# Gated cross-attention with a quantised feed-forward: inputs of feed-forward groups 2 to 4 transposed by DMA instead of TensorE

## The chip, the cores and the metric

The kernel runs on one core of one Trainium2 chip. The metric is device time in microseconds (us), the median of several executions. One execution is also recorded by the hardware profiler; all durations of single instructions come from that one.

## What is computed

The input x is 16 batches of 128 rows by 512 columns. A cross-attention block adds to it, and a feed-forward block adds to the result. The change lies in the second:

```python
x = x + jnp.tanh(g_xattn[0]) * _L0_xattn_ref(_layernorm(x, axis=-1), ctx_2048, ...)
x = x + jnp.tanh(g_ffn[0]) * _L0_ffn_ref(_layernorm(x, axis=-1), ...)

def _L0_ffn_ref(x, gate_up_packed, gate_up_scales, down_packed, down_scales):
    I = gate_up_packed.shape[0] // 2                       # 1408
    gate_up = jnp.einsum('bsh,oh->bso', x, w_gu)           # w_gu: fp4 values times scales
    gate, up = (gate_up[..., :I], gate_up[..., I:])
    h = jax.nn.silu(gate) * up
    y = jnp.einsum('bsi,hi->bsh', h, w_down)
    rms = jnp.sqrt(jnp.mean(y * y, axis=-1, keepdims=True) + EPS)
    return y / rms
```

## The kernel before

Attention takes the first 420 us. The feed-forward stage works on four groups of four batches (GROUP = 4), counted 0 to 3 in the code (g) and 1 to 4 in this text. Each group goes through IT = 11 steps, one for each 128 of the 1408 inner columns; T_ counts all 44 steps and t the step inside its group.

In a step TensorE does, in this order: 16 matmuls of 128x512 for gate and up (`gate_up`, L404, four input slices k, each with the head and the rest of the input in half precision), and 12 matmuls of 128x512 for the down product of step T_ - 2 (`project_down`, L420). Gate and up share four PSUM banks. ScalarE reads the gate banks (`take_gate`, L318), applies silu (L325) and makes the head of the hidden values (L331). VectorE reads the up banks (`take_up`, L167 and L170), multiplies (`join`, L175) and makes the rest of the hidden values (`hidden_rest`, L181). GpSimd adds the four gate parts (L299, L303).

Between these stands the work on the next and the last group, at fixed steps t: statistics of the next group (t = 1 to 4), its normalisation on GpSimd into `xn` (t = 5 and 6, `normalise`, L223), and for the last group the copy of y (t = 2), squares (t = 3, 4), the gain (t = 5) and the final sum on VectorE (`finish`, t = 6 to 9, L254), whose four results SyncE stores (`store`, L159).

The matmuls need the normalised input with its columns on the partitions, split into a half-precision head and a half-precision rest. Before the change this was done at t = 7 to 10 (TURN_AT = 7) for the next group: after the gate and up matmuls of the step TensorE transposes four 128x128 squares of `xn` into PSUM bank 0 (`turn_inputs`, L387), ScalarE copies the bank as the head (`input_head`, L335), VectorE subtracts the head from the bank (`input_rest`, L228), and the first gate matmul of the following step waits for that rest. There are two sets of head and rest tiles, used in turn. Each engine runs its instructions in the order of the code; semaphores tie the engines together. SyncE's queue holds, at the end of the attention, the last transfers of batch 15 and then the stores of the four groups.

Of the kernel before, what the change touches and what calls it, by code (L numbers as in the profile page):

```python
# [7 lines left out]
ALU = mybir.AluOpType  # L8
ACT = mybir.ActivationFunctionType
# [4 lines left out]
F16 = mybir.dt.float16  # L14
# [24 lines left out]
GROUP = 4  # L39
# [14 lines left out]
GROUPS = B // GROUP  # L54
# [4 lines left out]
H_RING = 3  # L59
STATS_AT, EVAC_AT, SQUARE_AT, ROOT_AT, NORM_AT, OUT_AT, TURN_AT = 1, 2, 3, 5, 5, 6, IT - KT  # L60
STEP_ROWS = 6
# [40 lines left out]
def feed_forward(nc, ctx, d, keep, tiles):  # L102
# [50 lines left out]

    turn_bank = lambda g, k: 0 if g else k

# [62 lines left out]
    def normalise(engine, ops, g, j):  # L218
        engine.wait_ge(negated, g + 1)
        engine.wait_ge(inv, g + 1)  # L220
        if g:
            engine.wait_ge(turned, g * KT)
        ops.tensor_scalar(xn[:, j, :], xg[g][:, j, :], neg_mean[:, j:j + 1], rstd[:, 1, j:j + 1],  # L223
                          ALU.add, ALU.mult).then_inc(normed, 1)

    def input_rest(dve, g, k):
        dve.wait_ge(x_heads, g * KT + k + 1)
        nc.vector.tensor_tensor(x_rest[g % 2][:, k], gu_ps[turn_bank(g, k)], x_head[g % 2][:, k], ALU.subtract).then_inc(x_rests, 1)  # L228

    def first_input_head(dve, k):  # L230
        dve.wait_ge(turned, k + 1)
        nc.vector.tensor_copy(x_head[0][:, k], gu_ps[turn_bank(0, k)]).then_inc(x_heads, 1)

# [23 lines left out]
    def vector_step(dve, T_):  # L257
# [11 lines left out]
        if T_ < NT:  # L269
            take_up(dve, T_, 3)  # L270
        if g + 1 < groups and t >= TURN_AT:
            input_rest(dve, g + 1, t - TURN_AT)
        if drains:
# [58 lines left out]

    def input_head(act, g, k):
        act.wait_ge(turned, g * KT + k + 1)
        nc.scalar.activation(x_head[g % 2][:, k], gu_ps[turn_bank(g, k)], ACT.Copy).then_inc(x_heads, 1)  # L335

# [13 lines left out]
    def scalar_step(act, T_):  # L350
# [9 lines left out]
        if T_ < NT:  # L360
            take_gate(act, T_, 2)
            take_gate(act, T_, 3)
        if g + 1 < groups and t >= TURN_AT:
            input_head(act, g + 1, t - TURN_AT)
        if drains:
# [14 lines left out]

    def turn_inputs(pe, g, k):
        if k == 0:
            pe.wait_ge(normed, (g + 1) * GROUP)
        if g:
            pe.wait_ge(gate_read, 4 * ((g - 1) * IT + TURN_AT + k) + 3)
        for j in range(GROUP):
            last = nc.tensor.transpose(gu_ps[turn_bank(g, k)][:, j * P:(j + 1) * P], xn[:, j, k * P:(k + 1) * P], keep["ident"][:])  # L387
        last.then_inc(turned, 1)

    def gate_up(pe, T_, n):  # L390
# [3 lines left out]
        at = 4 * T_ + k  # L394
        if t > TURN_AT and g + 1 < groups and n == 0:
            pe.wait_ge(x_rests, (g + 1) * KT + t - TURN_AT)
        elif at >= 2:
            pe.wait_ge(up_read if is_up else gate_read, at - 1)
        if T_ == 0 and n < KT:
            pe.wait_ge(x_rests, n + 1)  # L400
        elif t == 0 and n == 0:
            pe.wait_ge(x_rests, (g + 1) * KT)
        for moving, first in ((x_head, True), (x_rest, False)):
# [4 lines left out]
    def project_down(pe, T_):  # L408
# [3 lines left out]
        for j in range(GROUP):  # L412
# [14 lines left out]
            "turn_inputs": turn_inputs, "gate_up": gate_up, "project_down": project_down, "scalar_step": scalar_step,  # L427
            "last_squares": last_squares, "statistics": statistics, "normalise": normalise, "input_rest": input_rest,
            "first_input_head": first_input_head, "vector_step": vector_step, "last_finish": last_finish,
# [3 lines left out]
def attend(nc, d, keep):  # L433
    with ExitStack() as ctx:
# [115 lines left out]
        with ExitStack() as attention:  # L550
# [22 lines left out]
        with nc.Block() as block:  # L573
# [161 lines left out]
            def _(sp):  # L735
# [123 lines left out]
            def tensor_step(pe, b):  # L859
                for slot in range(SLOTS):  # L860
# [315 lines left out]
            def _(dve):  # L1176
# [171 lines left out]
```

## Time and profile before

| | |
|---|---|
| median of 3 runs | 721.06 us (720.33 to 721.33) |
| the profiled execution | 721.24 us, span of its instructions 719.4 us |
| TensorE busy | 688.7 us, 96% |
| VectorE busy | 610.1 us, 85% |
| ScalarE busy | 519.3 us, 72% |
| GpSimd busy | 476.3 us, 66% |
| mean granted TensorE clock | 0.974 of full speed |

Busy is the time in which an engine has an instruction at work. Matmuls are pipelined and overlap in the record, so how fast TensorE goes is better read from the distance between the same instructions of two steps. PEld is TensorE's loading of weights, which runs beside its matmuls (PE). An instruction's idle time, in brackets in a timeline, is how long its engine did nothing before it, with the instruction that ended the wait.

### The profile page before, as it was taken

What the parts mean: (1) busy time and instruction counts of PE and PEld (TensorE: products, weight loads), DVE (VectorE), ACT (ScalarE), POOL (GpSimd) and SP (SyncE); (2) the same over time, 40 slices, a digit from 0 to 9 for tenths busy, and PEclk for the clock granted to TensorE, in tenths of its full rate; (3) what the DMA queues carried; (4) which work ended last, traced back from release to release, by engine and by line L of the source; (5) the groups of instructions that cost most, each with busy time, mean ns of one, the idle gap of its engine ahead of it and who ended that gap; (6) DMA issues with size and microseconds to landing.
All of it is one profiled execution on the core that took longest, in us unless ns stands there. A gap on an engine that the chain in (4) does not pass through costs nothing.

```text
span 719.4 us, 13389 instructions
## 1 busy us (share of the span) xinstructions
PE 688.7 (96%) x4678; PEld 338.4 (47%) x4678; DVE 610.1 (85%) x825; ACT 519.3 (72%) x925; POOL 476.3 (66%) x403
## 2 busy tenths in 40 slices
PE   3779999999999999999999999999999999999995
PEld 2334434443444344434444344665565556555653
DVE  6788988988898889888989879776899789977894
ACT  1228888888888888888888976566666666666653
POOL 3857655796779766966633239976697669766773
PEclk8659999999999999999999999999999999999999
DMA  8787777778877877878663311000001000100001
GB/s 250 179 204 164 174 195 201 176 182 207 200 170 188 208 200 176 201 200 194 160 150 71 86 50 48 0 1 1 0 10 37 15 1 9 37 16 0 10 37 73
DMA packets 48935, 80.59 MB, mean 112 GB/s; under 512 B 14436, under 2 KB 17892, under 8 KB 48868
## 3 DMA queue, kind: packets, MB, share of 16 engines
q1 hardware_dynamic: 47712, 78.99, 43.7%
q10 hardware_dynamic: 1156, 0.74, 0.4%
q8 instruction: 37, 0.61, 0.4%
q14 instruction: 30, 0.25, 0.1%
HBM read 45.11 MB, written 32.24 MB: 108 GB/s over the span
## 4 chain that ended last, share of the span: by engine, by line
PE 48%; POOL 30%; issue 16%; DVE 3%; DMA 2%; ACT 1%; POOLq 0%; SPq 0%; DVEq 0%; ACTq 0%
PE pv_ps L845 18%; POOL probs L299 15%; PE s_ps L815 13%; POOL probs L303 9%; PE st_ps L827 8%; PE st_ps L788 2%; PE st_ps L800 2%; PE st_ps L857 2%; PE st_ps L794 2%; DVE max_rows L1119 1%; DMA qk_stack<-image 1%; POOL proj L1051 1%; POOL over_stack L223 1%; POOL proj L1046 1%; POOL cross L1044 1%
## 5 line engine op out<-in xcount | busy, mean ns | idle before, releaser
L1119 DVE TENSOR_REDUCE max_rows<-s_ps 128x2 f32<-128x1024 f32 x256 | 304.0, 1212 | 37.4 <-PE s_ps L815 36.7
L956 ACT ACTIVATE probs<-st_ps 128x512 f32<-128x512 f32 x512 | 278.1, 598 | 56.4 <-PE st_ps L827 46.0
L318 ACT ACTIVATE probs<-s_ps,gu_sc 128x512 f32<-128x512 f32 x176 | 117.7, 685 | 84.4 <-PE s_ps L404 84.2
L299 POOL TENSOR_TENSOR probs<-probs 128x512 f32<-128x512 f32 x88 | 120.3, 1371 | 69.5 <-ACT probs L318 69.3
L845 PE MATMUL pv_ps<-probs,v_all 128*32 128x256 f32 x2048 | 163.5, 392 | 0.6 <-ACT pv_all L962 0.6
L815 PE MATMUL s_ps<-qk_stack 48*128 48x512 f32 x512 | 132.7, 515 | 7.8 <-DVE max_rows L1119 5.3
L170 DVE SCALAR_TENSOR_TENSOR proj<-s_ps,gu_sc,proj 128x512 f32<-128x512 f32 x132 | 98.7, 748 | 11.1 <-PE s_ps L404 1.9
L827 PE MATMUL st_ps<-qk_stack 50*128 50x512 f32 x512 | 106.8, 405 | 0.0
L420 PE MATMUL st_ps<-dn_head,over_input 128*128 128x512 f32 x264 | 104.9, 423 | 1.0 <-DVE over_input L181 1.0
L815 PEld LDWEIGHTS s_ps<-qk_stack 48*128 48x128 f32 x512 | 49.3, 190 | 112.5 <-issue 73.8
L1081 POOL TENSOR_TENSOR heads_out<-pv_all,scale_of 128x512 f32<-128x512 f32 x16 | 20.5, 1282 | 98.0 <-DMA scale_of<-inverse_scratch 89.2
L404 PE MATMUL s_ps<-pv_all,gu_bits 128*128 128x512 f16 x352 | 80.1, 380 | 0.2 <-DVE proj L167 0.2
L845 PEld LDWEIGHTS pv_ps<-probs,v_all 128*32 128x32 f32 x2048 | 40.6, 108 | 84.3 <-ACT probs L956 59.9
L303 POOL TENSOR_TENSOR probs<-probs 128x512 f32<-128x512 f32 x44 | 71.3, 1622 | 3.5
L404 PE MATMUL s_ps<-split_head,gu_bits 128*128 128x512 f16 x176 | 66.9, 380 | 1.9 <-DVE proj L167 1.5
L827 PEld LDWEIGHTS st_ps<-qk_stack 50*128 50x128 f32 x512 | 64.8, 187 | 6.7 <-issue 3.4
L404 PE MATMUL s_ps<-split_rest,gu_bits 128*128 128x512 f16 x176 | 66.7, 379 | 0.0
L167 DVE TENSOR_SCALAR proj<-s_ps,gu_sc 128x512 f32<-128x512 f32 x44 | 32.8, 746 | 31.9 <-PE s_ps L404 31.8
L420 PEld LDWEIGHTS st_ps<-dn_head,over_input 128*128 128x128 f32 x264 | 49.6, 188 | 17.3 <-ACT over_input L331 1.4
L1044 POOL TENSOR_TENSOR cross<-proj,sin 128x1024 f32<-128x1024 f32 x15 | 35.7, 2379 | 30.0 <-ACT proj L946 27.2
L404 PEld LDWEIGHTS s_ps<-pv_all,gu_bits 128*128 128x128 fp8e3 x352 | 32.1, 98 | 43.4 <-issue 5.9
L420 PE MATMUL st_ps<-dn_rest,over_input 128*128 128x512 f32 x132 | 52.0, 394 | 0.0
(122 smaller groups left out, 892.2 us busy)
## 6 DMA issues: line engine op xcount, KB each, us to landing
qk_stack<-image SPq DMA_DIRECT2D x60, 384.0 KB, 6.4
image<-split_rest SPq DMA_DIRECT2D x32, 256.0 KB
image<-split_head SPq DMA_DIRECT2D x31, 256.0 KB
image<-split_head SPq DMA_DIRECT2D x62, 128.0 KB
xt_all<-x_dram SPq DMA_DIRECT2D x16, 256.0 KB, 3.6
ct<-ctx_dram SPq DMA_DIRECT2D x16, 256.0 KB, 3.6
scale_of<-inverse_scratch SPq DMA_DIRECT2D x16, 256.0 KB
out_dram<-over_stack SPq DMA_DIRECT2D x16, 256.0 KB, 2.0
```

The source lines that it names most:

```text
L170: nc.vector.scalar_tensor_tensor(out, bank, scale, out, ALU.mult, ALU.add).then_inc(up_read, 1)
L299: nc.gpsimd.tensor_tensor(pair[:, n], parts[T_ % 2][:, 2 * n], parts[T_ % 2][:, 2 * n + 1], ALU.add).then_inc(pairs_ok, 1)
L303: nc.gpsimd.tensor_tensor(gate[T_ % 2], pair[:, 0], pair[:, 1], ALU.add).then_inc(gate_ok, 1)
L318: nc.scalar.activation(parts[T_ % 2][:, k], gu_ps[(2 * k) % BANKS], ACT.Copy, scale=gu_sc[:, k, T_ % IT:T_ % IT + 1]).then_inc(gate_read, 1)
L404: last = nc.tensor.matmul(gu_ps[n % BANKS], gu_vals[:, k, col:col + P], moving[g % 2][:, k], start=first, stop=not first)
L420: last = nc.tensor.matmul(y_ps[j], h[T_ % H_RING][:, cols], keep[w][:, t, :], start=(t == 0 and n == 0), stop=(t == IT - 1 and n == 2))
L815: last = nc.tensor.matmul(out[:, odd, :], q_stack[p][rows, j, qt * P:(qt + 1) * P], k_stack[p][rows, j, :], start=True, stop=True)
L827: nc.tensor.matmul(out[:], k_stack[p][rows, j, kt * P:(kt + 1) * P], q_stack[p][rows, j, :], start=True, stop=True).then_inc(st_full, 1)
L845: last = nc.tensor.matmul(pv_ps[2 * KC * j:2 * KC * (j + 1), cols], v_ones[b % 2][:, kt, j, quad, :], probs[at % PROBS][:, j, cols], start ...
L956: nc.scalar.activation(probs[at % PROBS][:, tile % 4, :], st_ps[item % ST_BANKS][:], ACT.Exp).then_inc(st_read, 1)
L1044: ops.tensor_tensor(cross[:], tile[:], sin[:], ALU.mult).then_inc(crossed, 1)
L1119: nc.vector.tensor_reduce(out, s_ps[item % S_BANKS][:], AXIS_X, ALU.max).then_inc(s_read, 1)
```

## The change

For groups 2 to 4 TensorE's transposes into PSUM go. At t = 6 to 9 (SPLIT_AT = 6) ScalarE copies a batch of `xn` in half precision into `flat_head`, and VectorE subtracts that from `xn` into `flat_rest`, both in SBUF with the columns still along the row. SyncE then issues for each of the four batches four transposing transfers of 128x128 from `flat_head` and four from `flat_rest` into the head and rest tiles: 32 transfers in a group. The first gate matmul of the group waits until all 32 have landed. The order of SyncE's queue becomes: transposing transfers of group 2, those of group 3, stores of group 1, transfers of group 4, stores of group 2, stores of groups 3 and 4. The first group is still transposed by TensorE. `flat_head` and `flat_rest` lie over tiles that the attention stage used.

```diff
-STATS_AT, EVAC_AT, SQUARE_AT, ROOT_AT, NORM_AT, OUT_AT, TURN_AT = 1, 2, 3, 5, 5, 6, IT - KT
+STATS_AT, EVAC_AT, SQUARE_AT, ROOT_AT, NORM_AT, OUT_AT, SPLIT_AT = 1, 2, 3, 5, 5, 6, 6
...
-    turn_bank = lambda g, k: 0 if g else k
+    TURNS = 16 * 2 * KT * GROUP
...
     def normalise(engine, ops, g, j):
...
-        if g:
-            engine.wait_ge(turned, g * KT)
+        if g == 1:
+            engine.wait_ge(turned, KT)
+        elif g:
+            engine.wait_ge(flat_rests, (g - 1) * GROUP)
...
-    def input_rest(dve, g, k):
-        dve.wait_ge(x_heads, g * KT + k + 1)
-        nc.vector.tensor_tensor(x_rest[g % 2][:, k], gu_ps[turn_bank(g, k)], x_head[g % 2][:, k], ALU.subtract).then_inc(x_rests, 1)
+    def flat_input_rest(dve, g, j):
+        dve.wait_ge(flat_heads, (g - 1) * GROUP + j + 1)
+        if g >= 2:
+            dve.wait_ge(turned_in, TURNS * (g - 1))
+        nc.vector.tensor_tensor(flat_rest[:, j], xn[:, j, :], flat_head[:, j], ALU.subtract).then_inc(flat_rests, 1)
+
+    def turn_by_dma(sp, g):
+        sp.wait_ge(up_done, 4 * (g - 1) * IT)
+        for j in range(GROUP):
+            for out, flat, done in ((x_head, flat_head, flat_heads), (x_rest, flat_rest, flat_rests)):
+                sp.wait_ge(done, (g - 1) * GROUP + j + 1)
+                for k in range(KT):
+                    sp.dma_start(out[g % 2][:, k, j * P:(j + 1) * P], flat[:, j, k * P:(k + 1) * P], transpose=True).then_inc(turned_in, 16)
...
-        if g + 1 < groups and t >= TURN_AT:
-            input_rest(dve, g + 1, t - TURN_AT)
+        if T_ < NT and g + 1 < groups and SPLIT_AT <= t < SPLIT_AT + GROUP:
+            flat_input_rest(dve, g + 1, t - SPLIT_AT)
...
-    def input_head(act, g, k):
-        act.wait_ge(turned, g * KT + k + 1)
-        nc.scalar.activation(x_head[g % 2][:, k], gu_ps[turn_bank(g, k)], ACT.Copy).then_inc(x_heads, 1)
+    def flat_input_head(act, g, j):
+        act.wait_ge(normed, g * GROUP + j + 1)
+        if g >= 2:
+            act.wait_ge(turned_in, TURNS * (g - 1))
+            act.wait_ge(flat_rests, (g - 2) * GROUP + j + 1)
+        nc.scalar.activation(flat_head[:, j], xn[:, j, :], ACT.Copy).then_inc(flat_heads, 1)
...
-        if g + 1 < groups and t >= TURN_AT:
-            input_head(act, g + 1, t - TURN_AT)
+        if T_ < NT and g + 1 < groups and SPLIT_AT <= t < SPLIT_AT + GROUP:
+            flat_input_head(act, g + 1, t - SPLIT_AT)
...
-        if t > TURN_AT and g + 1 < groups and n == 0:
-            pe.wait_ge(x_rests, (g + 1) * KT + t - TURN_AT)
-        elif at >= 2:
+        if at >= 2:
             pe.wait_ge(up_read if is_up else gate_read, at - 1)
         if T_ == 0 and n < KT:
             pe.wait_ge(x_rests, n + 1)
-        elif t == 0 and n == 0:
-            pe.wait_ge(x_rests, (g + 1) * KT)
+        elif t == 0 and n == 0 and g:
+            pe.wait_ge(turned_in, TURNS * g)
...
+            "flat_head": magnitude[:].bitcast(F16)[:, 0:GROUP * T].rearrange("p (j t) -> p j t", t=T),
+            "flat_rest": dn_bits[:].bitcast(F16)[:, 0:GROUP * T].rearrange("p (j t) -> p j t", t=T),
...
                 for g in range(GROUPS):
-                    ffn["store"](sp, g)
+                    if g + 1 < GROUPS:
+                        ffn["turn_by_dma"](sp, g + 1)
+                    if g:
+                        ffn["store"](sp, g - 1)
+                ffn["store"](sp, GROUPS - 1)
...
-                if g + 1 < GROUPS and t >= TURN_AT:
-                    ffn["turn_inputs"](pe, g + 1, t - TURN_AT)
```

## Rows read from the trace of the kernel before

**Rows 1.** The page: busy time of two engines; TensorE's granted clock in 40 slices.
```profile
PE 688.7 (96%) x4678; PEld 338.4 (47%) x4678; DVE 610.1 (85%) x825; ACT 519.3 (72%) x925; POOL 476.3 (66%) x403
PEclk8659999999999999999999999999999999999999
```

**Rows 2.** Windows, busy us by engine: a plain step, and steps 18 and 19.
```profile
492.80:499.10 6.30, 6.30 (x30) 3.79 (x30) 4.52 (x6) 3.74 (x6) 3.97 (x4) 1.00 0.01 3
...
537.00:544.30 7.30, 6.94 (x34) 4.06 (x34) 6.91 (x8) 4.28 (x7) 7.14 (x7) 1.00 0.10 37
544.30:551.30 7.00, 6.80 (x33) 3.92 (x32) 6.79 (x10) 4.28 (x7) 5.09 (x4) 1.00 0.10 37
```

**Rows 3.** Timeline of weight loads: start us, duration; first loads of steps 6, 7, 11.
```profile
459.74 0.10 PEld L404 LDWEIGHTS s_ps<-split_head,gu_bits 128*128 128x128 fp8e3 x1 [0.27 <-issue]
...
466.01 0.10 PEld L404 LDWEIGHTS s_ps<-split_head,gu_bits 128*128 128x128 fp8e3 x1 [0.28 <-issue]
...
492.81 3.14 PEld L404 LDWEIGHTS s_ps<-pv_all,gu_bits 128*128 128x128 fp8e3 x16 [0.27 <-issue]
```

**Rows 4.** The same timeline, steps 17 to 22, loads that waited.
```profile
530.71 3.13 PEld L404 LDWEIGHTS s_ps<-pv_all,gu_bits 128*128 128x128 fp8e3 x16 [0.27 <-issue]
...
536.96 1.84 PEld L404 LDWEIGHTS s_ps<-pv_all,gu_bits 128*128 128x128 fp8e3 x10 [0.27 <-issue]
...
540.95 0.42 PEld L387 LDWEIGHTS s_ps<-ident,over_stack 128*128 128x128 f32 x4 [0.85 <-POOL over_stack L223]
...
544.25 1.84 PEld L404 LDWEIGHTS s_ps<-pv_all,gu_bits 128*128 128x128 fp8e3 x10 [0.28 <-issue]
546.79 0.54 PEld L404 LDWEIGHTS s_ps<-pv_all,gu_bits 128*128 128x128 fp8e3 x4 [0.69 <-DVE proj L167]
...
564.73 0.10 PEld L404 LDWEIGHTS s_ps<-split_head,gu_bits 128*128 128x128 fp8e3 x1 [0.27 <-issue]
```

**Rows 5.** Groups by form, 440 us to the end: count, busy us, mean ns.
```profile
L181 DVE TENSOR_TENSOR over_input<-cross,over_input 128x512 fp32r<-128x512 f32 x43 | 39.8, 925 | 1.7 <-ACT over_input L331 0.7
...
L254 DVE SCALAR_TENSOR_TENSOR over_stack<-over_stack,rms,xt_all 128x512 f32<-128x512 f32 x4 | 7.0, 1758 | 0.0
...
L335 ACT ACTIVATE pv_all<-s_ps 128x512 f16<-128x512 f32 x8 | 4.8, 597 | 1.7 <-PE s_ps L387 1.7
...
L254 DVE SCALAR_TENSOR_TENSOR over_stack<-st_ps,rms,xt_all 128x512 f32<-128x512 f32 x3 | 2.2, 747 | 0.1
```

**Rows 6.** Timelines of VectorE: step 9, then steps 17 to 22.
```profile
484.14 0.69 DVE L228 TENSOR_TENSOR pv_all<-s_ps,pv_all 128x512 f16<-128x512 f32 x1
...
531.79 0.75 DVE L167 TENSOR_SCALAR proj<-s_ps,gu_sc 128x512 f32<-128x512 f32 x1 [0.30 <-PE s_ps L404]
...
542.88 1.51 DVE L181 TENSOR_TENSOR over_input<-cross,over_input 128x512 fp32r<-128x512 f32 x1
...
546.00 0.74 DVE L167 TENSOR_SCALAR proj<-s_ps,gu_sc 128x512 f32<-128x512 f32 x1
...
550.22 0.68 DVE L181 TENSOR_TENSOR over_input<-cross,over_input 128x512 fp32r<-128x512 f32 x1
...
552.51 0.74 DVE L167 TENSOR_SCALAR proj<-s_ps,gu_sc 128x512 f32<-128x512 f32 x1
...
565.81 0.75 DVE L167 TENSOR_SCALAR proj<-s_ps,gu_sc 128x512 f32<-128x512 f32 x1 [1.75 <-PE s_ps L404]
```

**Rows 7.** Timeline of ScalarE: the last two gate copies of step 9.
```profile
482.02 1.31 ACT L318 ACTIVATE probs<-s_ps,gu_sc 128x512 f32<-128x512 f32 x2
```

**Rows 8.** SyncE's issues by line: ns min/median/max; landing after L646.
```profile
L159 SPq DMA_DIRECT2D out_dram<-over_stack x16: 332/332/377, 538.3 to 716.9; - x16
...
L646 SPq DMA_DIRECT2D pv_all<-pv_all x64: 571/589/1847, 77.9 to 427.9; - x64
DMA to landing us min/median/max: 1.9/3.2/4.7
...
L664 SPq DMA_DIRECT2D x_scratch<-xt_all x8: 533/990/1663, 119.2 to 287.3; - x8
```

More of the change, by code:

```diff
@@ L118, in feed_forward @@
     gu_ps, y_ps = tiles["gu_ps"], tiles["y_ps"]
+    flat_head, flat_rest = tiles["flat_head"], tiles["flat_rest"]
     rms = sb("rms", [P, 4, GROUP], F32)
@@ L127, in feed_forward @@
     turned = sem("turned3")
+    flat_heads = sem("flat_heads")
+    flat_rests = sem("flat_rests")
+    turned_in = sem("turned_in")
     x_heads = sem("x_heads")
@@ L220, in normalise, with first_input_rest @@
         engine.wait_ge(inv, g + 1)
-        if g:
-            engine.wait_ge(turned, g * KT)
+        if g == 1:
+            engine.wait_ge(turned, KT)
+        elif g:
+            engine.wait_ge(flat_rests, (g - 1) * GROUP)
         ops.tensor_scalar(xn[:, j, :], xg[g][:, j, :], neg_mean[:, j:j + 1], rstd[:, 1, j:j + 1],
                           ALU.add, ALU.mult).then_inc(normed, 1)
-    def input_rest(dve, g, k):
-        dve.wait_ge(x_heads, g * KT + k + 1)
-        nc.vector.tensor_tensor(x_rest[g % 2][:, k], gu_ps[turn_bank(g, k)], x_head[g % 2][:, k], ALU.subtract).then_inc(x_rests, 1)
+    def flat_input_rest(dve, g, j):
[10 more added lines that the diff above has]
+                    sp.dma_start(out[g % 2][:, k, j * P:(j + 1) * P], flat[:, j, k * P:(k + 1) * P], transpose=True).then_inc(turned_in, 16)
+    def first_input_rest(dve, k):
+        dve.wait_ge(x_heads, k + 1)
+        nc.vector.tensor_tensor(x_rest[0][:, k], gu_ps[k], x_head[0][:, k], ALU.subtract).then_inc(x_rests, 1)
     def first_input_head(dve, k):
         dve.wait_ge(turned, k + 1)
-        nc.vector.tensor_copy(x_head[0][:, k], gu_ps[turn_bank(0, k)]).then_inc(x_heads, 1)
+        nc.vector.tensor_copy(x_head[0][:, k], gu_ps[k]).then_inc(x_heads, 1)
     def wait_y(engine, g, j):
@@ L379, in last_squares, with turn_inputs @@
             square(act, groups - 1, j, y_ps[j])
-    def turn_inputs(pe, g, k):
+    def turn_inputs(pe, k):
         if k == 0:
-            pe.wait_ge(normed, (g + 1) * GROUP)
-        if g:
-            pe.wait_ge(gate_read, 4 * ((g - 1) * IT + TURN_AT + k) + 3)
+            pe.wait_ge(normed, GROUP)
         for j in range(GROUP):
-            last = nc.tensor.transpose(gu_ps[turn_bank(g, k)][:, j * P:(j + 1) * P], xn[:, j, k * P:(k + 1) * P], keep["ident"][:])
+            last = nc.tensor.transpose(gu_ps[k][:, j * P:(j + 1) * P], xn[:, j, k * P:(k + 1) * P], keep["ident"][:])
         last.then_inc(turned, 1)
@@ L427, in feed_forward @@
             "turn_inputs": turn_inputs, "gate_up": gate_up, "project_down": project_down, "scalar_step": scalar_step,
-            "last_squares": last_squares, "statistics": statistics, "normalise": normalise, "input_rest": input_rest,
+            "last_squares": last_squares, "statistics": statistics, "normalise": normalise, "first_input_rest": first_input_rest, "turn_by_dma": turn_by_dma,
             "first_input_head": first_input_head, "vector_step": vector_step, "last_finish": last_finish,
@@ L880, in tensor_step @@
                             pe.wait_ge(s_read, B * SLOTS)
-                        ffn["turn_inputs"](pe, 0, slot - FIRST_TURN)
+                        ffn["turn_inputs"](pe, slot - FIRST_TURN)
             def tensor_feed(pe, T_):
@@ L1217, in _ @@
                     ffn["first_input_head"](dve, k)
-                    ffn["input_rest"](dve, 0, k)
+                    ffn["first_input_rest"](dve, k)
                 dve.wait_ge(scales_ok, 2)
```

## The prediction

> **What bounds the kernel now.** The page first: TensorE is busy 96% of the span, VectorE 85%, and the granted clock is at its upper level in every slice but the first few [rows 1]. The change touches only the feed-forward stage, steps T_ = 0 to 43 from 422 us on, so the rest was read by step; groups are counted 1 to 4 here, steps by T_. The table of windows shows a plain step (492.8 to 499.1) with TensorE busy throughout and VectorE at 4.52 of 6.30 us, and steps T_ = 18 and 19 (537.0 to 551.3) in which VectorE fills 6.8 to 6.9 us and TensorE has gaps [rows 2]. I then took the start of each step from TensorE's weight loads: the load of the first gate matmul follows a short "issue" pause. Group 1: step 6 runs from 459.74 to 466.01, 6.27 us; the four steps with transposes from 466.01 to 492.81, 26.80 us or 6.70 each [rows 3]. A plain step is 6.25 us (530.71 to 536.96), so four transposes and their detour cost 0.45 us per step, bound by TensorE itself. In group 2 the same five steps run 530.71, 536.96, 544.25, 551.33 to 564.73, 34.02 us in all, where 5 x 6.25 + 4 x 0.45 would be 33.05. The difference has two names: the transposes of step 18 wait 0.85 us for GpSimd's normalised rows, and step 19 waits 0.69 us for VectorE to read a bank [rows 4]. I take group 3, which has the same work at the same t, to be alike.
>
> **What goes.** 48 transposes, four in each of twelve steps, with their copies out of PSUM. In group 1 VectorE has room, so the whole 4 x 0.45 = 1.8 us comes back. In groups 2 and 3 the bound is 34.02 - 31.25 = 2.8 us each, if TensorE alone sets the pace.
>
> **What VectorE and ScalarE do instead.** They execute as many splits as before, one step earlier, and now from SBUF: the head on ScalarE about 0.6 us [rows 5], the rest on VectorE. Of the rest's new form no row exists. Bounds: 0.69 us as now from PSUM [rows 6]; 0.92 us, the mean of L181, a TENSOR_TENSOR with both inputs in SBUF; 1.76 us, the time of L254 with both inputs in SBUF, against 0.75 when one is in PSUM [rows 5]. I take 0.69: L181 is the same operation and runs at 0.68 when nothing holds it [rows 6].
> The move matters in groups 2 and 3. VectorE's `finish` (1.76 us) stands in t = 6 to 9, the split in t = 7 to 10, so both meet in three steps now and in all four after. Such a step takes VectorE 552.51 - 546.00 = 6.51 us, more than TensorE's 6.25. From its first read of step 17 at 531.79, four of them end at 557.83. TensorE feels it when the first read, naturally 1.08 us into a step (565.81 against 564.73), starts after 1.35: the bank is wanted again ten matmuls or 2.2 us in, and the read takes 0.75. Step 21 would start at 530.71 + 25.0 = 555.71, so it is held 557.83 - 557.06 = 0.8 us, and step 22 starts at 562.8: 2.0 us gained. In step 18 L181 took 1.51 us instead of 0.68 [rows 6] while GpSimd was late with the normalisation; if that repeats, 1.1 us are gained. I take 1.4 per group, nearer to this end since GpSimd's work doesn't change, and 2.8 for two. Sum of the compute side: 1.8 + 2.8 = 4.6 us. The ends are 1.8 + 2 x 2.8 = 7.4 and, with the rest at 0.92 in four steps (0.9 less per group) and the slow step, 2.
>
> **What the transfers cost.** 32 transposing transfers per group are issued one by one by SyncE, each 128x128 in half precision, 32 KB. None is in the trace. They cost TensorE nothing if all have landed at the first gate matmul of the next group, the only wait that the change adds there; behind it on TensorE stand gate, up and down products, so every microsecond late is a microsecond of span. ScalarE ends its last gate copy 3.9 us into a step (482.02 + 1.31 = 483.3 against 466.01 + 2 x 6.70 = 479.4) and the head takes 0.6 [rows 7], so SyncE starts 4.5 us into t = 6; GpSimd's last normalised rows are there when the transposes of step 18 start, 540.95 [rows 4], ahead of the splits that need them in steps 19 and 20. SyncE's other waits, on up products of two groups back and on its own earlier transfers, are over by then. With a pace r per transfer and a landing L after the last issue, the last lands at 4.5 + 31r + L; group 1 allows 31.25 us, groups 2 and 3 32.6. What else bounds it: the last rest is ready 5.4 us into t = 9 (484.14 + 0.69 - 479.4 [rows 6]), with four transfers to issue and 12.5 - 5.4 = 7.1 us left.
> Rows for r: a plain 256 KB issue in this stage holds SyncE 0.33 us; the copies from SBUF to SBUF of 32 KB each, the nearest in place and size, 0.59 us, with a landing of 1.9 to 3.2; slow ones in the attention stage 0.99 (median of L664) to 1.85 (longest of L646) [rows 8]. With 0.59 and 3.2 the last lands at 26.0, and the tail rule gives 5.4 + 4 x 0.59 + 3.2 = 11.0 of 12.5 us: hidden. In this stage the queue is otherwise empty, which is why I take 0.59 and not the slow rows. Hidden holds up to r = 0.80 (L = 2.0). Beyond it each 0.1 us costs 3.1 us per group. All of the 4.6 us is eaten at about r = 0.87.
> Here the Trainium skill speaks with two voices. "VectorE: DVE Perf Modes", section "The three transpose paths", gives 1309 ns for one 128x128 transpose by DMA against 390 ns by TensorE; no run here shows whether that is a pace or a time to completion. As a pace it would put the last landing near 47 us and the time near 761, an estimate from that page. "Advanced Engine Details and Errata", section "X-Bar Transpose (TRN2)", says that such DMAs are as fast as regular ones, by which the sum above stands.
> **SyncE's queue.** The stores of group g - 1 now stand behind the transfers of group g + 1. Their first reader is ScalarE's square in step 36, which reuses `y_out` some fifteen steps later; the last group's stores have nothing new ahead of them. Nothing.
>
> **Sum.** The profiled execution took 721.24 us, 719.4 in its span and 1.8 around it, 0.2 above the median of the runs. 721.24 - 1.8 - 2.8 = 716.6.
>
> **Rivals.**
> - A, the forecast: r under 0.8, hidden, 716.6 us, from 714 (TensorE alone sets groups 2 and 3) to 719.5 (VectorE's splits at 0.92 and the slow step). For it: the 0.33 and 0.59 us issues, the empty queue. Against: a transposing issue is a different instruction.
> - B, slower: the transposing issue holds SyncE 1.0 to 1.85 us, and the first matmul of groups 2, 3 and 4 waits. It decides from r = 0.87. At the middle, 1.4: 4.5 + 43.4 + 2.0 = 49.9, so TensorE waits 18.6 + 17.3 + 17.3 = 53.2 us: 716.6 + 53.2 = 769.8. At 0.99 it is 732, at 1.85 812. For it: the rows of 0.99 to 1.85 us and 32 issues against 26.7 us; against: those came beside a busy queue. The clock after such pauses isn't priced.
> - C, in between: r = 0.9, 34.4 us, waits of 3.1 + 1.8 + 1.8: 723.4.
> - D, hidden, but VectorE becomes the bound: the rest from SBUF costs 1.76 us as L254 does, 1.07 more in 4 steps of 2 groups, 8.6 us: 725.2. Group 1 hides it: a step without `finish` leaves VectorE 1.75 us idle [rows 6]. Against: L181.
>
> **Chances.** A 0.48, B 0.34, C 0.10, D 0.08. A's own range is 714 to 719.5; both signs are likely, so the full range goes up to B at about r = 1.45, 775 us, and down to 714. A measurement can tell about 0.2% (1.4 us) from no change. Faster: A but 0.01, and 0.02 of C, 0.49. Same: 0.01 of A, 0.02 of C, 0.04 of D, 0.07. Slower: B, 0.06 of C, 0.04 of D, 0.44.
>
> **What would show it.** Steps 7 to 10 of 6.25 us in group 1; in groups 2 and 3, steps of about 6.5 with TensorE waiting on L170 or L167 of VectorE. The duration of the SyncE issues of the transposing transfers and the distance between them is r; the wait of the first gate matmul of a group on a DMA is B or C. The rest's duration at its new source tells A from D. I am wrong if the transfers land after TensorE's last down product of the group, or if heads and rests slow `hidden_rest` or GpSimd's additions, which share SBUF with them.

## The result, and the profile after

The changed kernel takes 767.58 us (median of four executions, 766.59 to 770.4) against 720.79 us before on the same chip: a ratio of 1.065, 95% interval 1.0633 to 1.0666, so 46.8 us slower. The forecast of 716.6 us had the wrong sign; the measured time lies inside the full range, which went up to 775. What happened is rival B, the wait on slow issues, with about 6 us more on the compute side, which D had named in part, and another 6 us from the clock. The profiled execution took 766.59 us, 764.8 of them in the span.

The page of the kernel after: the span, busy times, TensorE's busy tenths and granted clock in 40 slices, and two groups of gate and up matmuls.

```profile
span 764.8 us, 13405 instructions
PE 691.7 (90%) x4630; PEld 333.9 (44%) x4630; DVE 619.7 (81%) x825; ACT 520.3 (68%) x925; POOL 477.9 (62%) x403
PE   3789999999999999999999999659984998849996
PEclk8569999999999999999999999969998999969999
...
L423 PE MATMUL s_ps<-pv_all,gu_bits 128*128 128x512 f16 x352 | 85.1, 395 | 30.5 <-DMA pv_all<-dn_bits 27.1
...
L423 PE MATMUL s_ps<-split_head,gu_bits 128*128 128x512 f16 x176 | 68.0, 386 | 16.1 <-DMA split_rest<-dn_bits 10.9
```

TensorE's share fell from 96% to 90% [rows 1]. In its row there are three dents, one ahead of each of groups 2, 3 and 4, and the granted clock, which before stood at its upper level from the fourth slice to the end, has three dents in the same places. The releaser is named: DMA, the transposed rests.

The waits of the feed-forward stage, us in total, times, longest; then the issues of the transposing transfers by their line (ns min/median/max).

```profile
PE s_ps L423 <- DMA pv_all<-dn_bits: 27.1, 2, 14.9
...
PE s_ps L423 <- DMA split_rest<-dn_bits: 10.9, 1, 10.9
PE s_ps L423 <- DVE proj L171: 6.6, 8, 1.4
...
L244 SPq DMA_TRANSPOSE pv_all<-magnitude x32: 1106/1232/2460, 463.5 to 672.2; - x32
...
DMA to landing us min/median/max: 2.2/2.3/4.4
```

An issue holds SyncE for 1.23 us, not for the 0.33 to 0.59 of the plain ones in [rows 8]. The timeline of SyncE, group 1 (start, us, count): first and last four issues, and below, behind the last transfer for group 3 (in step 21), the stores of group 1.

```profile
463.55 5.03 SPq L244 DMA_TRANSPOSE pv_all<-magnitude  x4
...
499.87 5.05 SPq L244 DMA_TRANSPOSE pv_all<-dn_bits  x4
...
591.42 2.04 SPq L163 DMA_DIRECT2D out_dram<-over_stack  x4
```

Between two issues pass 1.275 us (5.10 us from one set of four to the next in an unbroken stretch). From 463.55 to 504.92 the queue is issuing with hardly a break. The last issue starts near 503.7 and lands 2.3 us later, at 506.0; the first matmul of group 2 starts at 506.16, after 14.95 us of idle time. The three waits of this kind add up to 38.0 us.

What the pause leaves behind: TensorE's first instructions of step 11, matmuls and then weight loads, and windows (us; busy time of PE, PEld, DVE, ACT, POOL; then granted clock, DMA share, GB/s) of a stretch inside the pause, of two stretches of step 11, and of the whole steps 11, 12, 22 and 33.

```profile
506.16 5.72 PE L423 MATMUL s_ps<-pv_all,gu_bits 128*128 128x512 f16 x16 [14.95 <-DMA pv_all<-dn_bits]
...
506.54 0.15 PEld L423 LDWEIGHTS s_ps<-pv_all,gu_bits 128*128 128x128 fp8e3 x1 [0.27 <-issue]
506.96 0.15 PEld L423 LDWEIGHTS s_ps<-pv_all,gu_bits 128*128 128x128 fp8e3 x1 [0.28 <-issue]
...
494.00:497.00 3.00, 0.00 (x0) 0.00 (x0) 0.00 (x0) 0.00 (x0) 0.00 (x0) 0.50 0.11 22
...
509.00:510.00 1.00, 1.00 (x4) 0.34 (x3) 0.24 (x1) 1.00 (x2) 0.33 (x1) 0.50 0.00 0
...
511.00:512.00 1.00, 1.00 (x7) 0.62 (x5) 0.95 (x2) 0.82 (x2) 0.00 (x0) 1.00 0.00 0
...
506.10:514.50 8.40, 8.34 (x28) 4.25 (x28) 4.53 (x6) 3.90 (x6) 3.44 (x3) 0.74 0.00 0
514.50:520.80 6.30, 6.30 (x30) 3.75 (x30) 4.94 (x7) 3.74 (x6) 4.23 (x4) 1.00 0.01 3
592.60:600.40 7.80, 7.79 (x28) 4.09 (x28) 4.51 (x6) 3.85 (x6) 3.44 (x3) 0.80 0.36 132
679.80:688.40 8.60, 8.59 (x29) 4.30 (x30) 4.53 (x6) 3.90 (x6) 3.48 (x3) 0.72 0.31 117
```

Step 11 does the work of a plain step with TensorE never idle, yet takes 8.36 us instead of 6.25: its weight loads last 0.15 us instead of 0.10 and follow each other at 0.43 us, where 16 of them took 3.14 us, 0.20 each, before [rows 3]. The clock fell inside the pause: it is at 0.50 from 494 on. So the step begins at the lower of the two levels (1.2 GHz), where it still is at 510, and from 511 on it is at the upper (2.4); its mean is 0.74, and the next step is at 1.00. Steps 22 and 33 do the same at 7.81 and 8.57 us. Together the three cost 2.1 + 1.5 + 2.3 = 5.9 us. TensorE did nothing while the clock fell, and the three pauses last 11 to 15 us; before the change, with no such pause, the clock is at 1.00 from 440 to 680 us.

The rest of the inputs in its new form, and the `hidden_rest` behind it, both on VectorE, grouped by form (count, busy us, mean ns).

```profile
L185 DVE TENSOR_TENSOR over_input<-cross,over_input 128x512 fp32r<-128x512 f32 x40 | 46.9, 1173 | 1.6 <-ACT over_input L351 0.7
...
L236 DVE TENSOR_TENSOR dn_bits<-over_stack,magnitude 128x512 f16<-128x512 f32 x12 | 13.5, 1127 | 0.0
```

The subtraction takes 1.13 us from SBUF, 0.69 before from PSUM [rows 6]; the hidden rest rose from a mean of 925 ns [rows 5] to 1173. Group 2 shows why. Timelines of VectorE and then of GpSimd where TensorE goes from step 17 to 18:

```profile
550.97 1.13 DVE L236 TENSOR_TENSOR dn_bits<-over_stack,magnitude 128x512 f16<-128x512 f32 x1
552.03 1.77 DVE L185 TENSOR_TENSOR over_input<-cross,over_input 128x512 fp32r<-128x512 f32 x1
553.71 1.75 DVE L274 SCALAR_TENSOR_TENSOR over_stack<-over_stack,rms 128x512 f32<-128x512 f32 x1
...
549.81 3.43 POOL L319 TENSOR_TENSOR probs<-probs 128x512 f32<-128x512 f32 x2
553.32 1.59 POOL L323 TENSOR_TENSOR probs<-probs 128x512 f32<-128x512 f32 x1
```

L185 ends at 553.80, 0.56 us after GpSimd's addition, which ended at 553.24 (549.81 + 3.43), and L274 ends at 555.46, 0.55 after L323 at 554.91. VectorE's instruction is done half a microsecond after the GpSimd one that runs beside it, whatever it had to do. All twelve subtractions from SBUF end 0.55 us after a GpSimd instruction; of the twelve from PSUM before the change none does.

The kernel before had such waits too: 26 of its last 40 hidden rests and all twelve sums of `finish` with both inputs in SBUF end 0.55 us after GpSimd. In ten of the twelve steps of the split the hidden rest escaped, because the subtraction ahead of it ended just as GpSimd changed from one addition to the next: in step 7 it began at 471.35, GpSimd's next addition at 471.40, and it took 0.68 us. GpSimd then waited instead: its addition L303 takes 1.73 to 1.78 us wherever a hidden rest began just ahead of it and about 1.60 nearly everywhere else. Now the subtraction ends too late for that gap, and in ten of the twelve cases the hidden rest sits out one more addition. Six of the twelve sums of `finish` gain by it, at 0.74 us instead of 1.76.

The time goes as follows. Steps 18, 19, 20 take 7.79, 7.26 and 7.01 us where before they took 7.29, 7.07 and 6.71, and group 1's steps 8 to 10 take 6.42, 6.71 and, without its DMA wait, 6.5. The compute side, measured alone below, is 6.0 us above the forecast. From the forecast: 716.6 + 6.0 (compute) + 38.0 (waits on transfers) + 5.9 (clock) = 766.5; the profiled execution took 766.59. That the sum closes to 0.1 us is partly chance, as the attention stage ahead differs by a microsecond from trace to trace. Counted from the first weight load of step 0, the feed-forward stage took 297.3 us before and takes 343.4; the kernel without transfers (298.9), the waits and the clock make 342.8 of them, and 0.6 us are left.

### The profile page after: what moved, and what is told of

Read it like the earlier page. It is cut to its first block, busy times and chain, and to the rows that moved or that the text cites. A ratio compares the mean times of both kernels' runs of the same rounds, so it can differ in the third digit from the quotient of the medians.

```text
span 764.8 us, 13405 instructions
## 1 busy us (share of the span) xinstructions
PE 691.7 (90%) x4630; PEld 333.9 (44%) x4630; DVE 619.7 (81%) x825; ACT 520.3 (68%) x925; POOL 477.9 (62%) x403
## 4 chain that ended last, share of the span: by engine, by line
PE 50%; POOL 25%; issue 18%; DVE 4%; DMA 1%; ACT 1%; POOLq 0%; ACTq 0%; DVEq 0%; SPq 0%
PE pv_ps L870 19%; POOL probs L319 15%; PE s_ps L840 14%; PE st_ps L852 8%; POOL probs L323 8%; PE st_ps L825 2%; DVE max_rows L1142 2%; PE st_ps L813 2%; PE st_ps L882 2%; PE st_ps L819 2%; DMA image<-split_head 1%; POOL over_stack L229 1%; DMA qk_stack<-image 1%; PE pv_ps L933 1%; POOL rms L212 0%
## 5 line engine op out<-in xcount | busy, mean ns | idle before, releaser
L319 POOL TENSOR_TENSOR probs<-probs 128x512 f32<-128x512 f32 x88 | 122.0, 1390 | 114.6 <-ACT probs L338 114.2
L423 PE MATMUL s_ps<-pv_all,gu_bits 128*128 128x512 f16 x352 | 85.1, 395 | 30.5 <-DMA pv_all<-dn_bits 27.1
L171 DVE TENSOR_SCALAR proj<-s_ps,gu_sc 128x512 f32<-128x512 f32 x44 | 32.8, 745 | 64.5 <-PE s_ps L423 64.5
L423 PE MATMUL s_ps<-split_head,gu_bits 128*128 128x512 f16 x176 | 68.0, 386 | 16.1 <-DMA split_rest<-dn_bits 10.9
L323 POOL TENSOR_TENSOR probs<-probs 128x512 f32<-128x512 f32 x44 | 69.7, 1584 | 3.5
L185 DVE TENSOR_TENSOR over_input<-cross,over_input 128x512 fp32r<-128x512 f32 x44 | 51.0, 1158 | 1.8 <-ACT over_input L351 0.7
```

The source lines that it names most:

```text
L185: nc.vector.tensor_tensor(h_rest[T_ % H_RING], hidden[T_ % 2], h_head[T_ % H_RING].bitcast(F32), ALU.subtract).then_inc(h_rests, 1)
L319: nc.gpsimd.tensor_tensor(pair[:, n], parts[T_ % 2][:, 2 * n], parts[T_ % 2][:, 2 * n + 1], ALU.add).then_inc(pairs_ok, 1)
L323: nc.gpsimd.tensor_tensor(gate[T_ % 2], pair[:, 0], pair[:, 1], ALU.add).then_inc(gate_ok, 1)
L423: last = nc.tensor.matmul(gu_ps[n % BANKS], gu_vals[:, k, col:col + P], moving[g % 2][:, k], start=first, stop=not first)
```

## The experiments

Two theories were tested. The issue theory: a transposing issue holds SyncE for 1.23 us whatever it carries; all 38 us of waits and the clock's 5.9 follow. Its rivals: the cost goes by the data moved, or the transfers in flight slow the engines. The turns theory: VectorE's SBUF instructions and GpSimd's wait for one another, and the moved subtraction adds one more to wait; its rivals are that the transfers disturb VectorE, and that the subtraction has its own fixed price.

The runs took place on several chips, each beside the kernel before on the same chip. The last column is the feed-forward stage in the trace, from the first weight load of step 0 to the end. It is the finer measure, because the attention stage, which no edit touches, took 420.7 to 423.5 us in these traces.

| kernel | time, us | before, same chip | ratio | stage, us |
|---|---|---|---|---|
| before | 720.79 | | | 297.3 |
| after | 767.58 | 720.79 | 1.065 | 343.4 |
| e_none | 722.59 | 721.2 | 1.0017 | 298.9 |
| e_wide | 722.81 | 721.2 | 1.0027 | 298.7 |
| e_heads (one execution) | 723.88 | 721.2 | | 298.9 |
| e_none_apart | 722.3 | 721.2 | 1.0011 | 297.6 |
| e_none_norest | 716.39 | 720.8 | 0.9936 | 291.9 |
| e_pool | 720.64 | 720.8 | 0.9989 | 297.3 |
| e_early | 715.42 | 721.33 | 0.9926 | 291.9 |
| e_early_narrow (one execution) | 738.45 | 721.33 | | 314.4 |
| e_none_copy | 720.72 | 720.73 | 1.0008 | 296.3 |

**e_none: the transfers removed**, with the waits on them; groups 2 to 4 multiply group 1's inputs.

```diff
-                for k in range(KT):
-                    sp.dma_start(out[g % 2][:, k, j * P:(j + 1) * P], flat[:, j, k * P:(k + 1) * P], transpose=True).then_inc(turned_in, 16)
...
-        elif t == 0 and n == 0 and g:
-            pe.wait_ge(turned_in, TURNS * g)
...
-            last = nc.tensor.matmul(gu_ps[n % BANKS], gu_vals[:, k, col:col + P], moving[g % 2][:, k],
+            last = nc.tensor.matmul(gu_ps[n % BANKS], gu_vals[:, k, col:col + P], moving[0][:, k],
```

> The changed kernel with all 96 transposing transfers and the waits on them left out; groups 2 to 4 multiply group 1's inputs, so these groups' results are not the right ones. What is left is the compute side of the change. The prediction's sum for it was 716.6 us. The theory after the trace of the changed kernel: VectorE's subtraction from SBUF (1.13 us) and the hidden rest behind it (1.76 instead of 0.68 to 1.0) wait for GpSimd, so group 1 gains 1.0 us and groups 2 and 3 lose 1.3 us each: 721.2 - 1.0 + 2.6 = 722.8 us, within 721.5 to 724. If the transfers themselves slowed the engines, steps 7 to 10 and 17 to 21 should come out shorter here than in the changed kernel.

722.59 us beside 721.2 before, ratio 1.0017 (1.0006 to 1.0027). So 45 of the 46.8 us come with the transfers (in the profiled executions, 766.59 and 722.61, 44.0: the 38.0 of waits and the 5.9 of the clock). But the gain of 4.6 us that the forecast saw on the compute side isn't there without them either: it is a loss of 1.4. Steps 18 to 20 take 7.78, 7.23 and 7.01 us, as in the full change, so the transfers aren't what slows them. VectorE, then GpSimd, at the end of step 19 of this kernel:

```profile
549.46 1.12 DVE L234 TENSOR_TENSOR dn_bits<-over_stack,magnitude 128x512 f16<-128x512 f32 x1
550.51 1.75 DVE L185 TENSOR_TENSOR over_input<-cross,over_input 128x512 fp32r<-128x512 f32 x1
552.19 0.74 DVE L270 SCALAR_TENSOR_TENSOR over_stack<-over_stack,rms 128x512 f32<-128x512 f32 x1
...
548.47 1.56 POOL L315 TENSOR_TENSOR probs<-probs 128x512 f32<-128x512 f32 x1 [1.42 <-ACT probs L334]
550.12 1.60 POOL L319 TENSOR_TENSOR probs<-probs 128x512 f32<-128x512 f32 x1
```

The subtraction ends 0.55 us after L315 (550.58 against 550.03), the hidden rest 0.54 after L319 (552.26 against 551.72). With GpSimd then out of the way, L270, which reads SBUF twice, takes 0.74 us instead of its 1.76 of [rows 5].

**e_wide: the same data in a quarter of the transfers.** One transfer turns 128x512, 8 a group.

```diff
-    TURNS = 16 * 2 * KT * GROUP
+    TURNS = 16 * 2 * GROUP
...
-                for k in range(KT):
-                    sp.dma_start(out[g % 2][:, k, j * P:(j + 1) * P], flat[:, j, k * P:(k + 1) * P], transpose=True).then_inc(turned_in, 16)
+                sp.dma_start(out[g % 2][:, :, j * P:(j + 1) * P], flat[:, j, :], transpose=True).then_inc(turned_in, 16)
```

> The changed kernel with one transposing transfer for each 128x512 (8 a group) in place of four of 128x128 (32 a group). If the 1.27 us is a cost of each instruction, SyncE is done 5 us after the last split, every wait is gone and the time is that of the kernel without transfers, 721.5 to 724 us. If the cost goes by the squares of 128x128 moved, an issue holds SyncE 4 x 1.23 = 4.9 us, and the time stays at 767 us; anything in between splits the 1.27 us into a fixed part and a part for each square.

The issues of its transfers (ns min/median/max) and their landing:

```profile
L243 SPq DMA_TRANSPOSE pv_all<-magnitude x8: 1189/1192/1725, 464.4 to 629.6; - x8
...
DMA to landing us min/median/max: 2.3/2.3/2.9
```

1.19 us for four times the data. The price belongs to the issue, not to the data, and no matmul waits on a DMA any more: 722.81 us, ratio 1.0027 (1.0015 to 1.0038), 0.2 us from the kernel that moves nothing.

**e_heads: sixteen transfers a group, in the small form.** Only the heads are transposed; all groups multiply the first group's rests.

```diff
-                for k in range(KT):
+                for k in range(KT if out is x_head else 0):
...
-        for moving, first in ((x_head, True), (x_rest, False)):
+        for moving, first in ((x_head, True), ((x_rest[0], x_rest[0]), False)):
```

> The changed kernel with only the heads transposed by transfers, 16 a group; the rests of groups 2 to 4 are those of group 1, so the results of these groups are off. If the pace of 1.27 us is all that makes the first matmul of a group wait, four issues take 5.1 us of a 6.25 us step, the last head lands about 4.5 + 3 x 1.27 + 2.3 = 10.6 us into t = 9 of 12.5, and no wait on a transfer is left: 721.5 to 724 us. If a transposing transfer costs the engines or the queue something beyond its pace, it is above that.

723.88 us in one execution, inside what was expected. No matmul waits on a DMA, and the stage takes 298.9 us as without transfers; the 1.3 us by which the span is longer (722.1 against 720.8) lie in the attention stage. Half the issues are hidden, which is what a pace of 1.275 us says: four of them take 5.1 us of a step of 6.25.

**e_none_apart: the subtraction pulled away from the hidden rest.** As e_none, with the subtraction one step later, between the first two reads of products.

```diff
+        if T_ < NT and g + 1 < groups and SPLIT_AT < t <= SPLIT_AT + GROUP:
+            flat_input_rest(dve, g + 1, t - SPLIT_AT - 1)
...
-        if T_ < NT and g + 1 < groups and SPLIT_AT <= t < SPLIT_AT + GROUP:
-            flat_input_rest(dve, g + 1, t - SPLIT_AT)
```

> The kernel without transfers (groups 2 to 4 multiply group 1's inputs), with VectorE's subtraction moved from just before the hidden rest to between the first two reads of PSUM banks in the next step. The theory that two neighbouring VectorE instructions with both inputs in SBUF must let a GpSimd instruction in between says that the hidden rest falls back from 1.76 to 0.7 to 1.0 us: group 1 runs at 6.25 us a step, groups 2 and 3 come 1 to 2 us under the kernel before, 716 to 719 us. The rival, that the subtraction is slow by itself and the hidden rest slow for another reason, leaves it at 722 to 724.

722.3 us, ratio 1.0011 (1.0001 to 1.0021), where e_none has 1.0017. By form, VectorE:

```profile
L185 DVE TENSOR_TENSOR over_input<-cross,over_input 128x512 fp32r<-128x512 f32 x37 | 35.9, 970 | 1.7 <-ACT over_input L348 0.5
L179 DVE TENSOR_TENSOR cross<-proj 128x512 f32<-128x512 f32 x38 | 32.3, 849 | 0.0
...
L234 DVE TENSOR_TENSOR dn_bits<-over_stack,magnitude 128x512 f16<-128x512 f32 x12 | 10.1, 845 | 0.0
```

Against e_none the hidden rest fell from a mean of 1190 to 970 ns and the subtraction from 1125 to 845, but the product of gate and up, `join` (L179), rose from 726 to 849. The wait moved to another instruction, and step 19 grew from 7.23 to 8.24 us. The expected gain of 3 to 6 us isn't there; the stage is 1.3 us shorter than e_none's.

**e_none_norest: the subtraction taken out.** As e_none, with a copy of two columns in its place.

```diff
-        nc.vector.tensor_tensor(flat_rest[:, j], xn[:, j, :], flat_head[:, j], ALU.subtract).then_inc(flat_rests, 1)
+        nc.vector.tensor_copy(flat_rest[:, j, 0:2], flat_head[:, j, 0:2]).then_inc(flat_rests, 1)
```

> The kernel without transfers (groups 2 to 4 multiply group 1's inputs), and VectorE's subtraction shrunk to a copy of two columns, so no rests are made for groups 2 to 4. If this subtraction and what it does to its neighbours is the whole of what keeps the compute side from its gain, group 1 runs at 6.25 us a step (1.8 us under the kernel before) and groups 2 and 3 are held only by finish, about 32.0 us for their five steps against 34.0: 721.2 - 1.8 - 4.0 = 715.4 us, within 714.5 to 716.5. If GpSimd's normalisation is what slows groups 2 and 3 (step 18 at 7.3 to 7.8 us), they stay at 33 us and more: 717.5 us or above.

716.39 us beside 720.8, ratio 0.9936 (0.9914 to 0.9957). Against e_none's 1.0017 that is 0.8%, 5.8 us for twelve instructions, 0.49 each; the stage in the two traces differs by 7.0. Steps 7 to 10 take 6.26 to 6.33 us, and step 18 takes 6.26. This is the time that the forecast had for the compute side, and it is reached with no subtraction, so the subtraction, with what it does to its neighbours, is what stood against it. Even two columns took 616 ns in the mean: the copy too waits for GpSimd, as all twelve end 0.03 us after a GpSimd addition. The hidden rest behind it then takes 0.68 us.

**e_pool: the subtraction on GpSimd.** As e_wide, with the subtraction moved to GpSimd, ahead of its additions in t = 8, 9 and 10 and, for the third tile, behind them in t = 9.

```diff
-        nc.vector.tensor_tensor(flat_rest[:, j], xn[:, j, :], flat_head[:, j], ALU.subtract).then_inc(flat_rests, 1)
+        nc.gpsimd.tensor_tensor(flat_rest[:, j], xn[:, j, :], flat_head[:, j], ALU.subtract).then_inc(flat_rests, 1)
...
+    REST_FIRST, REST_LAST = {8: 0, 9: 1, 10: 3}, {9: 2}
```

> The kernel with one transfer for each 128x512, with the subtraction that makes the rest moved from VectorE to GpSimd: at the start of its steps t = 8, 9 and 10, where it is idle for 1.3 to 1.9 us until the gate parts come, and one at the end of t = 9. The last rest is done about 2 us into t = 10, its transfer lands 2.3 us later, 2 us ahead of the first matmul that needs it. The theory that VectorE's share was the loss gives 6.25 us a step in group 1 and about 32 us for the five steps in groups 2 and 3: 715 to 717 us, a gain over the kernel before. The rival, that GpSimd's own instructions then delay VectorE by as much, because both take turns at the same inputs in SBUF, leaves it at 719 us or more.

720.64 us beside 720.8, ratio 0.9989 (0.9973 to 1.0006): not the gain expected. Group 1's steps 7 to 9 are at 6.25 us, but GpSimd comes late with its last subtraction, so the last transfers are late, and GpSimd, now busy for longer, holds VectorE's `join` (L179) instead. Waits, and a pair of VectorE and GpSimd instructions in step 19:

```profile
PE s_ps L427 <- DMA pv_all<-dn_bits: 2.2, 2, 1.1
...
PE s_ps L427 <- DMA split_rest<-dn_bits: 1.7, 1, 1.7
...
546.66 1.76 DVE L179 TENSOR_TENSOR cross<-proj 128x512 f32<-128x512 f32 x1
...
546.59 2.98 POOL L321 TENSOR_TENSOR probs<-probs 128x512 f32<-128x512 f32 x2
```

The three waits add up to 3.9 us; steps 20 and 21 take 7.43 and, with the wait of 1.7 us, 8.17 us. `join` lasts until 548.42, 0.55 us after the first of the two GpSimd instructions, which took 1.29 us.

**e_early: a version that beats the kernels before and after.** As e_pool, but for groups 3 and 4 the whole preparation starts with the last step before the previous group's first (statistics in t = -1 and 0, normalisation in 1 and 2, heads in 2 to 5, rests on GpSimd in 3 to 6), so that it no longer meets `finish`. For group 2 the four rests stand at t = 8 and 9, so that the last transfer lands in time. Both were changed at once, so the gain isn't divided between them.

```diff
+STATS_T = plan([(1, 0), (2, 1), (3, 2), (4, 3)], [(-1, 0), (-1, 1), (0, 2), (0, 3)])
+INVERT_T = plan([(4, 0)], [(0, 0)])
+NORM_T = plan([(5, 0), (5, 1), (6, 2), (6, 3)], [(1, 0), (1, 1), (2, 2), (2, 3)])
+HEAD_T = plan([(6, 0), (7, 1), (8, 2), (9, 3)], [(2, 0), (3, 1), (4, 2), (5, 3)])
+REST_START_T = plan([(8, 0), (9, 2)], [])
+REST_END_T = plan([(8, 1), (9, 3)], [(3, 0), (4, 1), (5, 2), (6, 3)])
```

> One transfer for each 128x512, subtraction on GpSimd, and for groups 3 and 4 statistics, normalisation and split moved up to t = -1 to 6, away from finish and from GpSimd's late steps; for group 2 the four rests at t = 8 and 9 so that the last transfer lands before t = 0. The theory that what was left of the loss in the kernel with the rests on GpSimd (steps 20 and 21 at 7.4 and 8.2 us, step 10 at 7.6) came from the rests meeting finish and the last transfer being late by 1.3 to 2 us, gives 6.25 us a step in group 1 (1.8 us gained) and 31.3 to 32 us for the last five steps of groups 2 and 3 (2.0 to 2.7 each), less up to 0.5 us each in the steps that got the work: 714 to 717 us. If the rests on GpSimd cost VectorE as much wherever they stand, it stays at 719 us or above.

715.42 us (714.77 to 717.58) beside 721.33: ratio 0.9926 (0.9911 to 0.9941). Steps 7 to 10 take 6.26 us, steps 18 to 21 take 6.34 to 6.37 where before they took 6.70 to 7.29, and no matmul waits on a DMA.

**e_early_narrow: the same with the 32 small transfers.**

```diff
-                sp.dma_start(out[g % 2][:, :, j * P:(j + 1) * P], flat[:, j, :], transpose=True).then_inc(turned_in, 16)
+                for k in range(KT):
+                    sp.dma_start(out[g % 2][:, k, j * P:(j + 1) * P], flat[:, j, k * P:(k + 1) * P], transpose=True).then_inc(turned_in, 16)
```

> The same with the 32 transfers of 128x128 for each group, as the change has them. If 1.27 us per issue is the whole cause of the waits, groups 3 and 4, whose first transfer now starts about 4.5 us into t = 2, have landed 41.9 us later, about 10 us before their first matmul, and show no wait at all; group 2, whose first starts at t = 6 as before, still waits about 15 us and pays about 2 us more for the lowered clock behind it: 730 to 735 us, against 767. If the transposing transfers disturb the engines while they run, groups 3 and 4 show longer steps than with the wide transfers.

738.45 us in one execution, 3 above the end of what was expected. Waits and SyncE's issues, group 1:

```profile
PE s_ps L443 <- DMA pv_all<-dn_bits: 19.9, 1, 19.9
...
464.36 5.03 SPq L262 DMA_TRANSPOSE pv_all<-magnitude  x4
474.25 5.13 SPq L262 DMA_TRANSPOSE pv_all<-dn_bits  x4
```

Groups 3 and 4, whose heads and rests are made four steps earlier, wait for nothing. Group 2 waits 19.9 us, not 15, since SyncE takes heads and rests in turn and stands from 469.4 to 474.25 for the first rest, 4.9 us in which nothing is issued. Step 11, after the pause, takes 8.65 us at a mean clock of 0.72: 715.4 + 19.9 + 2.4 = 737.7. Steps 17 to 21, with transfers in flight or just done, take 6.34 to 6.49 us beside e_early's 6.34 to 6.47, so no disturbance of the engines by the small transfers shows. The 738 us are also the price of the small form in the better kernel: 23 us above e_early for the same data.

**e_none_copy: one SBUF input instead of two.** As e_none, with a copy from single to half precision in place of the subtraction.

```diff
-        nc.vector.tensor_tensor(flat_rest[:, j], xn[:, j, :], flat_head[:, j], ALU.subtract).then_inc(flat_rests, 1)
+        nc.vector.tensor_copy(flat_rest[:, j], xn[:, j, :]).then_inc(flat_rests, 1)
```

> The kernel without transfers (groups 2 to 4 multiply group 1's inputs), with VectorE's subtraction of two SBUF tensors (1.13 us) replaced by a copy of one SBUF tensor of the same size and output type, so the rests of groups 2 to 4 are not rests. If VectorE waits for GpSimd only where it reads two tensors from SBUF, the copy takes 0.7 us or less each time, the hidden rest behind it falls back from 1.76 to 0.7 to 1.0 us, and the time is 716 to 718.5 us. If VectorE waits for GpSimd at any two neighbouring instructions on SBUF, the copy and the hidden rest stay at 1.1 and 1.76 us and the time at 722 to 724 us.

720.72 us beside 720.73, ratio 1.0008 (0.9984 to 1.0031). That lies between the two outcomes expected and fits neither. The medians can't tell it from e_none; in the traces the stage is 2.7 us shorter than e_none's, out of the 7.0 us that taking the subtraction out brought. VectorE, then GpSimd, at the end of step 19:

```profile
549.32 0.86 DVE L234 CAST dn_bits<-over_stack 128x512 f16<-128x512 f32 x1
550.10 1.76 DVE L185 TENSOR_TENSOR over_input<-cross,over_input 128x512 fp32r<-128x512 f32 x1
...
548.33 1.56 POOL L315 TENSOR_TENSOR probs<-probs 128x512 f32<-128x512 f32 x1 [1.19 <-ACT probs L334]
549.97 1.35 POOL L319 TENSOR_TENSOR probs<-probs 128x512 f32<-128x512 f32 x1
```

The copy too ends just after GpSimd's instruction (550.18 against 549.89), and the hidden rest behind it takes 1.76 us as before, ending 0.54 after L319 (551.86 against 551.32). The copy takes 0.86 us where the subtraction took 1.13, which is the part that comes back; the wait of the hidden rest doesn't. So waiting isn't a matter of two inputs alone: behind a copy as behind a subtraction, the hidden rest lets one GpSimd instruction through first.

## Why the prediction was wrong, point by point

- **The pace r of the transfers: mis-sized, and it decides all.** The formula (4.5 + 31r + L) held. With the measured r = 1.275 and L = 2.3 it gives 46.3 us against the 31.25 that group 1 allows, a wait of 15.1; the trace has 14.95. So close a fit is partly luck: the 31 paces took 40.1 us (503.69 - 463.55), not 39.5, and the five steps took 32.2, not 31.25. The failed step is "I take 0.59": a row of a plain copy of the same size stood in for another kind of instruction. Size and place don't set the price; the kind does (e_wide: 1.19 us for four times the data). The 1309 ns for one 128x128 transpose by DMA in the Trainium skill, "VectorE: DVE Perf Modes", section "The three transpose paths", agrees with the trace as a pace of issues (1.275 us). The Trainium skill, "Advanced Engine Details and Errata", section "X-Bar Transpose (TRN2)", says that such DMAs are as fast as regular ones: the trace agrees in the landing (2.3 us against 1.9 to 3.2) and not in the issue (1.23 against 0.33 to 0.59).
- **The waits of groups 3 and 4.** The formula gives 46.3 - 32.6 = 13.7 us each; the trace has 10.9 ahead of group 3, since the compute steps beside it were 2.8 us longer than taken, and 12.2 (27.1 - 14.9) ahead of group 4, where one issue took 2.46 us.
- **The clock after the pauses** was named and not priced: 5.9 us, 13% of the loss.
- **The rest on VectorE: mis-sized.** Taken at 0.69, it is 1.13 us. The 0.68 of L181 was read where it started at 550.22 [rows 6], between two of GpSimd's additions (the next began at 550.28); in 26 of 40 cases it took 1.0 us or more. More than that, the step missed the neighbour: the hidden rest behind the subtraction goes from 0.68 up to 1.76 us in these steps. D had the engine right and one of the two instructions, at 1.76 instead of 1.13; it stood 8.6 us above the forecast, measured were 6.0.
- **Rival B's middle, 769.8 us, lies 2 us from the measured time by luck.** It held r = 1.4 and 53.2 us of waits, where 1.275 and 38.0 came; the compute side and the clock, which it left out, made up 11.9 of the 15.2.
- **Group 1's steps.** 6.25 us forecast for all four; only step 7 has it. Steps 8 to 10 take 6.4 to 6.7, 0.9 us more in all. The claim that VectorE has room there is right for its own busy time and wrong for what it waits for: with no subtraction (e_none_norest) they take 6.26 to 6.33.
- **Groups 2 and 3.** VectorE as the bound was right (L171 is what TensorE waits for, 6.6 us), four steps of 6.51 us were not: 7.0 to 7.8.
- **Right.** The head's 0.6 us on ScalarE; the start of SyncE 4.5 us into t = 6 (463.55 - 459.03); the landing, 2.3 us inside the 2.0 to 3.2 taken; SyncE's stores behind the transfers, which cost nothing.

The turns of VectorE and GpSimd are also a rule of the Trainium skill ("SBUF — State Buffer", section "Who interferes with whom"): a VectorE instruction with two SBUF inputs, or a copy or cast of the fast modes, and a GpSimd instruction that reads SBUF lock each other out for a whole instruction. The trace agrees from both sides, with ends 0.55 us behind GpSimd's, a little less than the 0.68 that the instruction takes alone, and with GpSimd's 1.73 to 1.78 us instead of 1.60. The row of rival D already showed it: L254 at 1758 ns with both inputs in SBUF against 747 with one in PSUM [rows 5].

**What stays open.** Whether the 1.23 us is spent in SyncE itself or in what makes the transfer's descriptors isn't separated. Transfers wider than 128x512 weren't tried. The turns were shown by their end times and by taking the VectorE instruction away; taking GpSimd's additions away was not tried, so that one lets the other through is read from the timelines. Why e_none_apart and e_pool gained so little was read from one pair of instructions each, and not tested.

## What to carry to other kernels

Price a kind of DMA that isn't in the trace by measuring one of it, since here a neighbour of the same size was off by a factor of two, and put as much as you can into one transposing transfer: the issue costs 1.2 us whether it turns one square or four. Before an operation's source moves from PSUM to SBUF, look at what GpSimd runs beside it and which instruction stands behind it. A long wait on TensorE can cost more than itself: each of the waits of 11 to 20 us here cost 1.5 to 2.4 us of clock on top. And a formula for what can be hidden is only as good as the pace put into it: here a single measured issue would have turned the forecast round.

## What the runs showed of the hardware

- A transposing transfer holds SyncE 1.23 us (128x128) or 1.19 us (128x512), at a pace of 1.275, and lands in 2.3 us.
- After pauses of 11 to 20 us of TensorE the next step runs at a mean granted clock of 0.72 to 0.80 and takes 1.5 to 2.4 us more than 6.25.
- VectorE's instructions with two inputs in SBUF end 0.55 us after the GpSimd instruction beside them: 1.13 us for a 0.7 us subtraction, 1.76 for the one behind it. One that starts between two GpSimd instructions takes 0.68, and GpSimd's next then takes 1.73 to 1.78 instead of 1.60. A copy of two columns takes 0.62 us.
